# A fused cross-attention, self-attention and feed-forward block: the causal mask added by VectorE, and the softmax exponential issued head by head on ScalarE

## What is computed

```python
scores = jnp.einsum('bqhd,bkhd->bhqk', q, k) * scale
causal = jnp.tril(jnp.ones((s, s), dtype=scores.dtype))
scores = scores + (1.0 - causal) * MASK_VAL
probs = jax.nn.softmax(scores, axis=-1)
ctx = jnp.einsum('bhqk,bkhd->bqhd', probs, v).reshape(b, s, e)
x = x + _L0_attn_ref(_layernorm(x, axis=-1), ...)
```

## Time and profile before

| | before |
|---|---|
| median of 3 runs | 644.33 us |
| the profiled execution's own time | 645.53 us |
| its span | 643.9 us |
| PE (TensorE matmul) busy | 604.1 us, 94% |
| DVE (VectorE) busy | 448.6 us, 70% |
| ACT (ScalarE) busy | 297.6 us, 46% |
| granted TensorE clock, mean | 0.986 |
| chain that ended last, share of PE | 81% |

### The profile page before, as it was taken

The page is one execution under the profiler, slowest core; times in us unless marked ns, Lnnn a source line. Parts: engine busy times, 40 slices in busy tenths (PEclk is TensorE's granted clock), DMA queues, the critical chain, the costliest instruction groups (busy, mean ns, idle before and its releaser), DMA issues.

```text
span 643.9 us, 12627 instructions
## 1 busy us (share of the span) xinstructions
PE 604.1 (94%) x4832; PEld 299.6 (47%) x4832; DVE 448.6 (70%) x897; ACT 297.6 (46%) x374; POOL 11.1 (2%) x20
## 2 busy tenths in 40 slices
PE   1669987999999999999999999999999999899997
PEld 0234442454545555554445455544544554354453
DVE  7599995779747854885586568537865569767661
ACT  5888765774455545545634554555331233101010
POOL 3000000000000000000000000000000000000000
PEclk9879999999999999999999999999999999899999
DMA  9999896862284156317712751463240062023221
GB/s 320 385 388 383 331 301 235 280 227 70 98 263 164 67 195 213 115 65 259 258 69 84 251 186 65 168 219 103 98 163 2 1 212 97 35 78 119 84 79 49
DMA packets 38878, 109.17 MB, mean 170 GB/s; under 512 B 4026, under 2 KB 4282, under 8 KB 38848
## 3 DMA queue, kind: packets, MB, share of 16 engines
q1 hardware_dynamic: 37072, 104.35, 46.3%
q0 software_dynamic: 1344, 4.23, 1.7%
q10 hardware_dynamic: 432, 0.18, 0.1%
HBM read 100.35 MB, written 8.39 MB: 169 GB/s over the span
## 4 chain that ended last, share of the span: by engine, by line
PE 81%; DVE 11%; DMA 3%; SPq 2%; ACT 1%; issue 1%; DVEq 0%; ACTq 0%
PE dense L1104 16%; PE dense L1106 15%; PE dense L1105 15%; PE cross L1141 7%; PE turn L1095 6%; DVE wq L774 4%; PE dense L1235 4%; PE dense L1236 4%; PE dense L1237 4%; PE score L1198 2%; SPq L532 2%; DMA wq<-in_ctx 2%; PE score L1222 2%; DMA lnt<-in_ctx 1%; PE dense L1117 1%
## 5 line engine op out<-in xcount | busy, mean ns | idle before, releaser
L1104 PE MATMUL dense<-wq,xn_h 128*128 128x512 f16 x400 | 152.4, 381 | 0.0
L1105 PE MATMUL dense<-wq,xn_h 128*128 128x512 f16 x400 | 151.9, 380 | 0.0
L1106 PE MATMUL dense<-wq,xn_l 128*128 128x512 f16 x400 | 151.9, 380 | 0.0
L318 ACT ACTIVATE code<-raw,cst,qc 128x1024 uint8<-128x1024 f32 x74 | 90.2, 1237 | 17.9 <-DMA raw<-in_ctx 17.1
L1141 PE MATMUL cross<-code,q1t 128*128 128x512 f16 x256 | 74.7, 393 | 8.5 <-ACT code L318 4.2
L1106 PEld LDWEIGHTS dense<-wq,xn_l 128*128 128x128 f16 x400 | 39.2, 98 | 47.5 <-issue 0.6
L1104 PEld LDWEIGHTS dense<-wq,xn_h 128*128 128x128 f16 x400 | 39.2, 98 | 40.8 <-issue 2.8
L1105 PEld LDWEIGHTS dense<-wq,xn_h 128*128 128x128 f16 x400 | 39.3, 98 | 37.8 <-issue 0.9
L334 ACT ACTIVATE at<-turn 128x512 f32<-128x512 f32 x32 | 19.1, 597 | 76.8 <-PE turn L1095 76.0
L318 ACT ACTIVATE code<-lnt,cst,qc 128x1024 uint8<-128x1024 f32 x34 | 42.1, 1238 | 26.9 <-DMA lnt<-in_ctx 19.9
L803 DVE TENSOR_REDUCE smx<-score 128x8 f32<-128x512 f32 x32 | 22.0, 686 | 44.0 <-PE score L1198 44.0
(11 more groups left out here) (159 smaller groups left out, 935.8 us busy)
## 6 DMA issues: line engine op xcount, KB each, us to landing
raw<-in_ctx SPq DMA_DIRECT2D x74, 512.0 KB, 4.8
lnt<-in_ctx SPq DMA_DIRECT2D x34, 512.0 KB, 4.3
wo<-in_ctx SPq DMA_DIRECT2D x12, 512.0 KB, 9.1
wo<-in_qkv_w SPq DMA_DIRECT2D x12, 512.0 KB, 12.3
wq<-in_ctx SPq DMA_DIRECT2D x8, 512.0 KB, 11.5
wq<-in_qkv_w SPq DMA_DIRECT2D x8, 512.0 KB, 12.1
x_scratch<-xb SPq DMA_DIRECT2D x8, 512.0 KB, 3.2
wq<-x_scratch SPq DMA_DIRECT2D x8, 512.0 KB, 3.7
```

The source lines that it names most:

```text
L318: act.activation(low_bytes, src, ACT.Identity, scale=qc[:, 1:2], bias=z2).then_inc(s_u8, 1)
L1104: pe.matmul(bank[:, :], a_h[:, k, :], w_hi, start=(k == 0 and not started), stop=False)
L1105: pe.matmul(bank[:, :], a_h[:, k, :], w_lo, start=False, stop=False)
L1106: ins = pe.matmul(bank[:, :], a_l[:, k, :], w_hi, start=False, stop=(k == KC - 1 and not last))
```

## The change

Pair 0 keeps the code of before. For pairs 1 to 7:

- `scores` has no mask matmuls; each small product starts its own accumulation.
- `softmax_in` adds the mask on VectorE while it moves the scores from PSUM to `pr` (one scalar_tensor_tensor), then takes the negated maximum of each head from `pr` in SBUF. TensorE is released from `score` by a new semaphore `s_msk` behind the first of the two.
- `exponent` issues 8 Exp instructions of 128 x 64, one per head, each with its head's negated maximum as bias and with its sum kept by `accum_out`.
- `softmax_out` has no sum any more.
- ScalarE's list: exponent 1 now stands ahead of q(12), in pairs 1 to 6.

```diff
             def exponent(i, g):
                 act.wait_ge(s_sub, 4 * i + g + 1)
-                act.activation(pr[:, g % 2, :], pr[:, g % 2, :], ACT.Exp).then_inc(s_exp, 1)
+                if not masked_by_vector(i):
+                    act.activation(pr[:, g % 2, :], pr[:, g % 2, :], ACT.Exp).then_inc(s_exp, 1)
+                    return
+                for h in range(HPG):
+                    one = pr[:, g % 2, h * SEQ:(h + 1) * SEQ]
+                    ins = act.activation(one, one, ACT.Exp, bias=smx[:, g % 2, h:h + 1], accum_out=ssum[:, g % 2, h:h + 1])
+                ins.then_inc(s_exp, 1)
...
                 q(10, 11)
                 w(30)
                 exponent(i, 0)
+                exponent(i, 1)
                 q(12)
-                exponent(i, 1)
                 q(13)
                 qk_evac(i, 2)
...
                 dve.wait_ge(s_sc, 4 * i + g + 1)
+                if masked_by_vector(i):
+                    dve.wait_ge(s_pt, 4 * i + g - 1)
+                    dve.scalar_tensor_tensor(p3, mask_rows, MASK_SEL, s3, ALU.mult, ALU.add).then_inc(s_msk, 1)
+                    dve.wait_ge(s_msk, 4 * i + g - 3)
+                    dve.tensor_reduce(smx[:, g % 2, :], p3, AX.X, ALU.max, negate=True).then_inc(s_sub, 1)
+                    return
...
                 dve.wait_ge(s_exp, 4 * i + g + 1)
-                link(dve.tensor_reduce(ssum[:, g % 2, :], p3, AX.X, ALU.add))
+                if not masked_by_vector(i):
+                    link(dve.tensor_reduce(ssum[:, g % 2, :], p3, AX.X, ALU.add))
...
+            def read_by_softmax(i, count):
+
+                if masked_by_vector(i):
+                    pe.wait_ge(s_msk, 4 * i - 4 + count)
+                else:
+                    pe.wait_ge(s_sub, 4 * i + count)
...
-                for n in range(2):
-                    rows = slice(n * SEQ, (n + 1) * SEQ)
-                    pe.matmul(S[n][:, :], row_of[rows, :], mask_rows[rows, :, :], start=True, stop=False)
+                vector = masked_by_vector(i)
+                if not vector:
+                    for n in range(2):
+                        rows = slice(n * SEQ, (n + 1) * SEQ)
+                        pe.matmul(S[n][:, :], row_of[rows, :], mask_rows[rows, :, :], start=True, stop=False)
```

More of the change, by code:

```diff
@@ L193, in build @@
         s_sub = sem("s_sub")
+        s_msk = sem("s_msk")
         s_exp = sem("s_exp")
@@ L227, in build, with masked_by_vector @@
         bias_low_stage = rope[:, 1, :].bitcast(F16)
+        def masked_by_vector(i):
+            return not isinstance(i, int) or i > 0
         def above(value):
@@ L990, in _ @@
             x_low(0, 1)
-            per_pair = 2 * STATS_LINKS + 4 + 2 + 3 * GROUPS
+            per_pair = 2 * STATS_LINKS + 4 + 2 + GROUPS
             def run(i):
@@ L1185, in scores @@
                 if half:
-                    pe.wait_ge(s_sub, 4 * i + 2)
+                    read_by_softmax(i, 2)
                 elif above(4 * i):
                     pe.wait_ge(s_cl, 4 * i)
-                for n in range(2):
-                    rows = slice(n * SEQ, (n + 1) * SEQ)
-                    pe.matmul(S[n][:, :], row_of[rows, :], mask_rows[rows, :, :], start=True, stop=False)
+                vector = masked_by_vector(i)
[3 more added lines that the diff above has]
+                        pe.matmul(S[n][:, :], row_of[rows, :], mask_rows[rows, :, :], start=True, stop=False)
                 for m in range(4):
@@ L1198, in scores @@
                             ins = pe.matmul(S[n][par * SEQ:(par + 1) * SEQ, col:col + SEQ], qkt[rows, 2 * half, c:c + SEQ],
-                                            qkt[rows, 2 * half + 1, c:c + SEQ], start=False, stop=(m == 3 and b == 1))
+                                            qkt[rows, 2 * half + 1, c:c + SEQ], start=vector, stop=vector or (m == 3 and b == 1))
                             if m == 3 and b == 1 and par:
@@ L1212, in values_due @@
                 else:
-                    pe.wait_ge(s_sub, 4 * i + 4)
+                    read_by_softmax(i, 4)
             def values(i, half):
```

## The result

| | before | changed |
|---|---|---|
| median | 644.86 us (4 runs, 643.79 to 647.0) | 668.78 us (4 runs, 668.2 to 669.98) |
| the profiled execution's own time | 645.53 us | 669.19 us |
| its span | 643.9 us | 667.5 us |
| PE busy | 604.1 us | 606.0 us |
| DVE busy | 448.6 us | 430.7 us |

The changed kernel takes 1.0366 times the time of before (95% interval 1.0343 to 1.039). It was forecast slower, by 16.9 us; it is slower by 23.9 us (23.7 between the two profiled executions). The time lies in the range of 647 to 679, 7.6 us above the forecast of 661.2: the slowdown is 7.0 us larger than the sum, and the kernel before came out 0.5 us higher than the median that the forecast started from.

A forecast was written before the change was run, and what follows sets the result against it. TensorE was taken to bound the kernel, busy 59.48 of 59.52 us in pair 3. Terms - 4.5 + 16.3 + 5.1 = + 16.9 us gave 662.4 against the profiled 645.53, so a median of 661.2 us; range 647 to 679.

The forecast's parts named there:

- the sum: Whole kernel: mask saving and two TensorE waits added, - 4.5 + 16.3 + 5.1 = + 16.9 us.
- The mask's removal: TensorE ahead of the scores: two mask matmuls fewer save 0.32 us per half, 4.5 us over 14 halves.
- The step from one Exp to the next: ScalarE's Exp by head: 0.245 us start to start plus 0.08 for the accumulator output, e = 0.33.
- rival B: ScalarE's Exp: the accumulator read waits for the Exp to end, e = 0.42, sum + 34.2 us, 678.5; chance 0.20.
- rival A: ScalarE's Exp: the accumulator output is free, e = 0.245, sum + 3.6 us, 648.0; chance 0.20.
- rival C: ScalarE's Exp by head is cheap, e under 0.207; at 0.155 the kernel gains 4.1 us, 640.2; chance 0.07.
- The wait at p_turn: First half: TensorE waits for qk_evac 2, 2.62 us in pairs 2 to 6, 3.17 in pair 1, together 16.3.
- Rival D: At p_turn: q(12), q(13) hold back nothing, TensorE's wait had another cause; + 0.6 us, 644.9; chance 0.03.
- the order of exponent 1 and q(12): ScalarE's list: moving exponent 1 ahead changes nothing, since both stand ahead of the evacuation either way.
- The wait at x_turn: Second half: VectorE's norm comes late, TensorE waits 0.85 us in pairs 1 to 6, 5.1 us.
- VectorE's removed sums cost and bring nothing: VectorE behind the exponential: 28 instructions fewer, costed at nothing, as TensorE does not wait for VectorE there.
- The clock: TensorE: idle time lowering the granted clock was named as a way to be wrong, but priced at nothing.

The follow-up runs named there:

- experiment 2: The changed kernel with the quantisations q(12) and q(13) moved behind p_evac 1 in ScalarE's list: 649.18 us, 1.006 times before.
- experiment 4: The kernel before with only four ScalarE copies of 128 x 896 added ahead of qk_evac 2 in pairs 2 to 6: 661.25 us, 1.0243 times before.
- experiment 1: The changed kernel with exponent 1 put back behind q(12) in ScalarE's list: 670.14 us, 1.0388 times before.
- experiment 6: The changed kernel with sums on VectorE instead of accum_out, and q(12), q(13) behind p_evac 1: 641.95 us, 0.9948 times before.
- experiment 3: The changed kernel without accum_out, the sums of the heads taken by VectorE again: 648.56 us, 1.0069 times before.

## Why the forecast was right in kind and 7 us short

**The mask's removal** saves 0.32 us per half, as counted, and the gap of 0.31 us ahead of the scores stayed.

**The step from one Exp to the next** was forecast at 0.33 us and measured 0.333, in parts of 0.240 and 0.093 where the forecast had 0.245 and 0.08. The terms that the prediction lists for the first part (0.12, 0.03 and 0.09) add up to 0.24, not 0.245; the slip and the short 0.08 offset each other, which is luck on a small scale. The read is an instruction of its own on ScalarE as it was on VectorE, and the read of 187 ns mostly overlaps its neighbours, so rival B (0.42) falls; so do rival A, whose 0.245 needed the read to be free, and rival C, which needed 0.207 or less.

**The wait at p_turn** was forecast at 2.62 us and is 2.63. In pair 1 TensorE comes 3.50 us late there (3.92 us behind its neighbour instead of 0.42), where 3.17 were forecast. The other 0.33 were overlooked: in pair 1 ScalarE starts the first Exp straight behind its own work (138.43 in the earlier trace rows, 138.92 now), and not when VectorE releases it. So the 0.32 us that TensorE saves on the mask ahead of this place bring the Exp no earlier, and TensorE waits them away. Experiments 2 and 4 show from both sides that it is ScalarE's list ahead of qk_evac 2: take two quantisations out and 0.4 us are left of it, put four copies in and it comes. Rival D falls by this. That the order of exponent 1 and q(12) does not matter was right (experiment 1).

**The wait at x_turn** was forecast at 0.85 us and is 0.93.

**VectorE's removed sums cost and bring nothing** held: VectorE waits for ScalarE where they stood. So there is room for them: where ScalarE is relieved of the read (experiment 6), the sums fit back into VectorE and the kernel is fastest.

**The clock is the step that failed.** The prediction's last sentence set it at nothing, as a fall for which "no row here gives a reason", and the sum was made at a full clock. The trace of the kernel before does hold the reason, at two places outside the loop that the prediction's rows left out. TensorE waits 2.57 us ahead of the x_turn of pair 1 and 2.23 us in the third step, behind pair 7, and soon after each the clock is at its lower level for somewhat over 3 us:

```profile
109.53 1.10 PE L1095 MATMUL turn<-cst,lnt 128*128 128x128 f32 x8 [2.57 <-DVE lnt L764]
550.73 0.39 PE L1281 MATMUL cross<-code 128*128 128x512 f16 x1 [2.23 <-DVE wq L835]
```

```profile
112.00:114.00 2.00, 2.00 (x3) 0.75 (x3) 1.87 (x3) 0.00 (x0) 0.00 (x0) 0.50 0.93 303
552.00:554.00 2.00, 2.00 (x6) 0.75 (x5) 1.38 (x3) 0.72 (x2) 0.00 (x0) 0.50 0.00 0
```

The first two rows are TensorE's timeline. The other two have the columns of the stretches above; the 0.50 behind the last bracket is the granted clock, half of 2.4 GHz. So this trace had falls of the clock behind waits of the very size that the sum brings out.

A pair at a full clock is 62.49 us, against a forecast of 62.4. But three of the five pairs from 2 to 6 ran for somewhat over 3 us at 1.2 GHz behind the long wait, about 1.66 us each, 5.0 in all. Pair 1 is 5.3 us longer than before (64.90 from x_turn to x_turn against 59.60), where the forecast's terms make 3.4 (3.17 + 0.85 - 0.64). Its granted clock from 142 to 152 us is 0.83 against 1.00, one fall more than before; by the price of the others that is about 1.7 us, and the 0.33 at p_turn are the rest, within 0.1 us. So the slowdown of 16.9 us grows by 5.0 + 1.7 + 0.3 to 23.9, beside 23.7 between the two profiled executions. That sum is closer than its parts deserve. Five waits at x_turn are 0.08 us longer each, the x_turn of pair 1 came 0.5 us later, and the time behind pair 6 is 1.9 us shorter where 0.64 were due, as that part of the kernel before had a fall of the clock (0.97 from 550 to 600 us) and the changed one had none. These nearly cancel, by luck.

## What to carry to other kernels

When one engine is full and another half idle, look not at the busy shares but at the places where the full engine takes something from the other's in-order list, and count what stands in that list ahead of each. One instruction of 128 x 512 that becomes eight of 128 x 64 costs by its starts: 0.24 us each here, 0.33 with an accumulator. Where a sum brings out a new wait of TensorE like the 2.6 us here, look in the trace of before for the clock behind waits of that size, wherever they stand, and price it too, here by 1.66 us for each time that it falls; and where an addition is unavoidable, move work that is due later behind the thing that is waited for, which was worth 19.6 us here.

## What was not expected of the hardware

Waits of TensorE of 2.67 us in the changed kernel, and of 2.35 to 2.90 us in the kernel before with nothing but a delay added, brought the granted clock from 2.4 to 1.2 GHz for somewhat over 3 us in three of five pairs each. Their length did not decide which: in the delayed kernel 2.43 us brought it and 2.72 us did not. Waits of 0.4 to 1.2 us brought it in none of the ten pairs 2 to 6 of experiments 2 and 3. That is no safe length, though: in pair 0 of experiment 6 two waits of 1.26 and 0.80 us stand close together, TensorE is busy for 1.95 of the 4 us from 86 to 90, and the clock falls there too (0.50 from 90 to 92 us). The accumulator output of ScalarE is a row of 187 ns of which 93 ns are paid.
